# A graph kernel's gather pass over groups of 512 edges in place of 1024, with rings of eight smaller slots

## What is computed

```python
x = x + L0(h)     # sum over edges of h[src] * W
x = x + L1(h)     # two mean aggregations with weights between
x = x + L2(h, edge_attr)
x = x + L3(h)     # mean over edges of h[src] @ W.T + b
```

```python
eh = edge_h @ W_fcr.T
alpha = _segment_softmax(eh, dst, N)
z = h[src]
agg = jax.ops.segment_sum(alpha * (z + eh), dst, num_segments=N)
h_new = jnp.where((deg > 0)[:, None], agg + h @ loop_W, h)
return jax.nn.relu(h_new)
```

## Time and profile before

| | us |
|---|---|
| median of 3 runs (lowest, highest) | 6717.57 (6715.99, 6721.05) |
| the profiled execution, its own time | 6711.77 |
| its span, first to last instruction | 6709.9 |
| gather pass, first to last gather issue | 4275.6 to 6428.4 |
| busy over the span: PE, PE weight loads, DVE, ACT, POOL | 5183.6, 4649.6, 4620.1, 3754.5, 3317.2 |

### The profile page before, as it was taken

One profiled execution on the slowest core, in us unless ns is written; L12 is line 12 of the kernel. 1 busy time (PEld: TensorE's weight loads), 2 busy tenths in 40 slices (PEclk: granted clock), 3 DMA queues, 4 the chain that ended last, 5 costly groups with the idle time before them and its releaser, 6 DMA issues.

```text
span 6709.9 us, 129361 instructions
## 1 busy us (share of the span) xinstructions
PE 5183.6 (77%) x47386; PEld 4649.6 (69%) x47387; DVE 4620.1 (69%) x6392; ACT 3754.5 (56%) x3088; POOL 3317.2 (49%) x3412
## 2 busy tenths in 40 slices
PE   0046548888888849999989999656888878888886
PEld 0011137777777749999989999656777767777776
DVE  9846648888888877888878888434555555555554
ACT  0101137777777757887867878203545545454565
POOL 0477777777777720000010000377777777777730
PEclk9978769999999979999999999878999999999998
DMA  9998997777778766666666666335777767776785
GB/s 347 353 233 262 280 289 241 237 241 237 238 242 242 226 149 186 200 195 192 197 175 193 202 195 195 107 82 126 157 150 157 153 140 153 150 155 149 159 139 113
DMA packets 1691085, 1314.11 MB, mean 196 GB/s; under 512 B 920210, under 2 KB 1555091, under 8 KB 1690031
## 3 DMA queue, kind: packets, MB, share of 16 engines
q1 hardware_dynamic: 872085, 948.47, 48.1%
q10 hardware_dynamic: 705808, 299.82, 19.2%
q0 software_dynamic: 112592, 57.76, 5.3%
HBM read 833.36 MB, written 311.54 MB: 171 GB/s over the span
## 4 chain that ended last, share of the span: by engine, by line
PE 41%; DVE 6%; ACT 5%; issue 5%; DMA 3%; POOL 3%; DVEq 2%; SPq 0%; ACTq 0%; POOLq 0%
PE pair L1719 23%; PE pair L1839 8%; PE wide L1863 6%; ACT u L1613 3%; POOL u L1200 3%; ACT batch L1613 2%; DVE u L967 1%; DMA extra<-hi_b,tsel 1%; DMA u<-zrows,stage 1%; PE wide L1902 1%; DMA u<-cells 1%; DVEq L421 1%; DVE batch L1032 1%; ACT u L1450 0%; DVE u L623 0%
## 5 line engine op out<-in xcount | busy, mean ns | idle before, releaser
L1719 PE MATMUL pair<-tab,u 128*128 128x192 bf16 (+1 forms) x29106 | 2527.5, 247 | 114.9 <-ACT u L1450 110.6
L1719 PEld LDWEIGHTS pair<-tab,u 128*128 128x128 bf16 x29106 | 2459.7, 98 | 134.6 <-ACT u L1450 113.7
L1450 ACT ACTIVATE u<-u 128x1792 bf16<-128x1792 uint8 (+1 forms) x1360 | 2270.6, 1701 | 388.2 <-PE pair L1719 209.2
L1200 POOL DMA_INDIRECT u<-zrows,stage x1664 | 1608.7, 967 | 1329.0 <-DMA zrows<-batch 784.0
L1165 POOL DMA_INDIRECT cells<-val,idx x1664 | 1618.3, 973 | 742.9 <-issue 492.5
L623 DVE TENSOR_REDUCE u<-u 128x1792 bf16<-128x1792 uint8 (+1 forms) x838 | 1673.5, 2020 | 351.1 <-PE pair L1719 250.6
L1839 PE MATMUL pair<-u 128*128 x4880 | 937.5, 350 | 412.7 <-DVE u L967 395.8
L1839 PEld LDWEIGHTS pair<-u 128*128 128x128 f32 x4880 | 854.1, 203 | 488.4 <-issue 487.0
L1613 ACT ACTIVATE u<-u 128x1792 bf16<-128x1792 uint8 x317 | 524.9, 1684 | 316.0 <-PE wide L1863 309.5
L1679 PE MATMUL wide<-u,wbd 128*128 128x512 f32 x840 | 514.0, 702 | 194.1 <-DVE u L732 102.6
L1863 PE MATMUL wide<-u 128*128 128x193 bf16 x5544 | 521.4, 246 | 37.4 <-ACT u L1613 31.1
(11 more groups left out here) (284 smaller groups left out, 4363.4 us busy)
## 6 DMA issues: line engine op xcount, KB each, us to landing
u<-cells SPq DMA_DIRECT2D x2100, 224.0 KB, 3.1
cells<-zt SPq DMA_DIRECT2D x100, 1568.0 KB, 15.7
u<-in_ea SPq DMA_DIRECT2D x420, 256.0 KB
ex_d<-u ACTq DMA_DIRECT2D x420, 256.0 KB
u<-ex_d SPq DMA_DIRECT2D x208, 512.0 KB
u<-gate_d SPq DMA_DIRECT2D x420, 64.1 KB
u<-gate_d ACTq DMA_DIRECT2D x420, 64.0 KB
cells<-val,idx POOLq DMA_INDIRECT x1664
```

The source lines that it names most:

```text
L1200: pool.indirect_dma_start(out=ring3[:, slot, k, :], out_offset=None, in_=zrows, in_offset=bass.IndirectOffsetOnAxis(ap=stage[:, st, c:c + ...
L1450: return S.activation(to, of, ACT.Copy)
L1719: mm = M(acc(p, t // 2 * 2 + b)[:, 0:width], ring[:, q % nr, (b * CK + k) * P:(b * CK + k + 1) * P], table[:, j, 0:width], start=j == 0 an ...
```

## The change

`CH` goes from 8 to 4 and with it the group from 1024 to 512 edges (416 groups); the rings `ring3` and `exr` get eight slots of half the size, so that they hold the same 32 columns; SP loads seven groups ahead in place of three, POOL waits for the landing four groups back in place of two. A group's halves become two columns. `SG`, `GET_AT` and `ADD_AT` are doubled, so they name the same edges. In the scatter the half groups of four columns, which were the unit of three in flight (`DEEP`), become the groups themselves. Two small tables change their place (`below`, `ends`).

```diff
-CH = 8
+CH = 4
 GE = CH * P
 G = -(-E // GE)
-SLOTS = 4
-SG = 8
+SLOTS = 8
+SG = 16
...
-XR = 4
+XR = 8
...
-        shared = sb("shared", [P, max(GPK * T, STEPS + 1)])
-        below = shared[0:GP, 0:GPK * T].rearrange("p (a t) -> p a t", a=GPK)
-        ends = shared[:, 0:STEPS + 1]
+        below = hi_b[0:GP, 0:GPK * T].rearrange("p (a t) -> p a t", a=GPK)
+        ends = sb("ends", [P, STEPS + 1])
...
-        GET_AT, ADD_AT = 20, 60
+        GET_AT, ADD_AT = 40, 120
...
-                for h in range(2 * g, 2 * g + 2):
-                    if h >= DEEP:
-                        done(h - DEEP)
-                    for k in range(CH // 2):
-                        c = h * (CH // 2) + k
-                        pool.indirect_dma_start(out=spots, out_offset=bass.IndirectOffsetOnAxis(ap=idx[:, c:c + 1].bitcast(u32), axis=0),
-                                                in_=val[:, c:c + 1], in_offset=None).then_inc(scat[h % DEEP], 16)
-
-            def done(h):
-                pool.wait_ge(scat[h % DEEP], CH // 2 * 16 * (h // DEEP + 1))
-                if h % 2:
-                    pool.sem_inc(scat_done, 1)
+                if g >= DEEP:
+                    done(g - DEEP)
+                for c in range(g * CH, (g + 1) * CH):
+                    pool.indirect_dma_start(out=spots, out_offset=bass.IndirectOffsetOnAxis(ap=idx[:, c:c + 1].bitcast(u32), axis=0),
+                                            in_=val[:, c:c + 1], in_offset=None).then_inc(scat[g % DEEP], 16)
+
+            def done(g):
+                pool.wait_ge(scat[g % DEEP], CH * 16 * (g // DEEP + 1))
+                pool.sem_inc(scat_done, 1)
...
-                if g >= 2:
-                    pool.wait_ge(landed[(g - 2) % SLOTS], CH * 16 * ((g - 2) // SLOTS + 1))
+                if g >= 4:
+                    pool.wait_ge(landed[(g - 4) % SLOTS], CH * 16 * ((g - 4) // SLOTS + 1))
```

More of the change, by code:

```diff
@@ L1179, in _ @@
                     list_add(0, g - ADD_AT)
-            for h in range(2 * G - DEEP, 2 * G):
-                done(h)
+            for g in range(G - DEEP, G):
+                done(g)
             heads_add(0)
```

## The result

The changed kernel takes **6939.4 us** (median of 6 runs, 6933.4 to 6945.1), the kernel before beside it 6719.3 (6 runs, 6715.7 to 6728.8): a ratio of 1.0329, 95% interval [1.0318, 1.0339]. It is slower by 220 us, as forecast (6937).

What follows compares the result with a forecast made beforehand. Turns 1 to 6 were taken as bound by the consumers' one-group-at-a-time chain, turn 0 by POOL. 380.9 - 109.2 - 44.5 - 4 - 3 = +220 us on 6717.6 gave 6937 us, range 6880 to 7020.

Steps and rivals of the forecast that it cites:

- The chain step: Gather pass, turns 1 to 6: each further group of a tile costs 2.42 us through SP, DVE and PE, before 2.95.
- SP's issue takes 0.36 and I leave it: Within a step, SP's load issue keeps its 0.36 us; if it halved, a step were 0.18 less.
- The steps in all: Turns 1 to 6: 272 steps of 2.42 us replace 94 of 2.95, +380.9 us.
- ends of the pass: Last seven groups of the gather pass need no load ahead: four steps about 1 us shorter, -4 us.
- The closing group: Each of 84 tiles' last group in turns 1 to 6: eight PE passes instead of 16, -109.2 us.
- The opening: Opening group to first further group, 84 tiles: DVE's product and compare shrink by 0.53 us, -44.5 us.
- Turn 0: First turn of the gather pass: stays bound by POOL's gathers, only the last group's work shrinks, -3 us.
- the list additions come nearer together: Scatter pass: additions some 6.6 us apart, but one lands in 4.24 us, so no wait, 0 us.
- Rival 1: POOL or PE paces turns 1 to 6, SP's release does not gate: faster, 6660 to 6675 us; chance 0.07.
- Rival 2: No change: added steps hide under something else, such as ACT's casts; 6705 to 6731 us, chance 0.03.
- Rival 3: PE idles in each step and loses its clock in the groups: slower still, 7030 to 7300 us; chance 0.07.
- Rival 4: Small DVE operations save nothing: step stays 2.95 us, opening unchanged, 7126 us; chance 0.03.

Runs made afterwards that it cites:

- e1: Changed kernel with SP's load issued one group later in its loop, six groups ahead in place of seven: 6752.8 us, ratio to before 1.0053.
- e4: Changed kernel with each load of expanded edges issued from SP as two DMAs of half the size, same bytes: 7082.9 us, ratio to before 1.0543.
- e3: Changed kernel with the scatter pass's eight list additions behind every second group of four scatters, not every group: 6928.1 us, ratio to before 1.0311.
- e5: Changed kernel with four slots and four rows of edge inputs in place of eight and eight: 6973.0 us, ratio to before 1.0379.

## Why the prediction was right, and where its terms were off

**The chain step** (2.42 us forecast, 2.41 measured) and its parts. By the tile above: PE's start to the product 5460.11 to 5461.57 = 1.46 (forecast 0.62 + 0.84), product to compare 0.34 (0.61 - 0.265), compare to PE 0.61 (0.42 + 0.20). What doesn't depend on the size did stay, and the two operations shrank as the straight line said. e1 and e4 show that the part through SP is on the path: moving the load out takes 0.72 us from each step, a second load adds 0.52. "SP's issue takes 0.36 and I leave it" was right, too: a load of half the elements is issued in 0.360 us, as in the earlier trace rows.

**The steps in all**: +380.9 forecast, 662.8 - 288.4 = +374.4 measured. The 94 steps of before cost 288.4 us, not 277.3: I multiplied by the typical 2.95, and their mean is 3.07, since six of them, one a turn and all in its eighth tile, behind a norm chain, take 4.5 to 5.3. The 272 came to 662.8, not 658.2. The **ends of the pass** (-4, four steps about 1 us shorter) are in these 662.8: the last five steps of the pass take 1.69 to 1.73, some 0.7 less than the others, -3.6 in all.

**The closing group**: -109.2 forecast, 117.7 - 226.2 = -108.5 measured. **The opening**: -44.5 forecast, 331.6 - 383.3 = -51.7 measured, 0.62 us each in place of 0.53. In the tile above the path from product to PE falls by 0.57 (1.53 in the earlier trace rows, 0.96 now), and the product itself starts 0.16 earlier behind the opening group's start (1.87 in the earlier trace rows, 1.71 now); the second part I had not counted, and what brings it is not settled.

**Turn 0** had -3 and gave -0.8. **POOL's wait for slots** grew off the path, as forecast; **loop entries** at 0 and the **clock** at 0 held: the step came out at its forecast, and the clock at 0.94 as before.

**The step that failed**: "the list additions come nearer together ... but one lands in 4.24 us, so no wait: 0". The last scatter came 12.8 us later, and e3 shows the additions to be the cause of nearly all of it. The addition of the earlier trace rows belongs to a later list, in another stage. Here the first five land in 7.75 to 9.03 us, longer than the spacing of some 6.6 us that I had worked out. The trace of before could have told it: there a scatter that stands 8.23 us behind an addition is put down to that addition's landing.

```profile
902.12 1.59 POOL L1140 DMA_INDIRECT extra<-hi_b,tsel  x1 [0.30 <-issue]
910.35 0.96 POOL L1165 DMA_INDIRECT cells<-val,idx  x1 [0.30 <-DMA extra<-hi_b,tsel]
```

The scatters beside it are not what makes the difference. Before, the eight additions of this list all stand among scatters, 12 us apart, and by their semaphore the first four land in 8.0 to 8.8 us, the last four in 4.7 to 5.9. What falls between them is the load on the DMA engines (trace of before, columns as in the earlier trace rows; the share of busy DMA time is the last but one, and a full load reads about 1):

```profile
915.00:930.00 15.00, 3.67 (x10) 2.14 (x10) 3.81 (x5) 2.45 (x4) 11.65 (x12) 0.61 1.02 343
...
955.00:970.00 15.00, 9.12 (x26) 5.10 (x24) 8.57 (x12) 3.65 (x6) 11.65 (x12) 0.50 0.77 221
```

In the changed kernel, too, the last three, from 932.9 on, land in 6.0, 3.5 and 3.6 us, and nothing waits for them. No run changes the load alone, so it is a reading of the traces.

So the sum against the profiled execution was 10 us short (220 for 230), and the median came out nearly on the forecast because the two profiled executions lie 10 us further apart than the medians: that part of the agreement is luck.

**The rivals.** Rival 1 asked for a step below 1.61 us for any gain. With the late load the step is 1.69 in the median and 1.76 in the mean (479.9 / 272), and turns 1 to 6 take 1891 us, 30 more than before; with four pieces it is 1.60 and 1.68 (456.2 / 272), and they take 1866, 5 more. The point at which it turns was about right; the changed kernel stands far on the other side. That PE is the fullest engine decided nothing: its passes fell and the time rose. Rival 2 went with the time itself, 220 us longer. Rival 3 did not come about: with PE idle for 0.85 us ahead of a step, as in the tile above, the granted clock of turns 1 to 6 is 0.94, as before. The Trainium skill (TensorE: Matmul & The Clock Gate, "A second HAM failure mode: psum-queue depth-cycling") tells of a kernel in which short idle times of PE between groups made the clock swing between its two levels. These idle times brought no such loss. In e5, behind 4.19 us without a weight load, the clock did fall (last section). Rival 4 is refuted by the two groups of 0.427 and 0.417 us.

## What to carry to other kernels

Where several engines pass one group at a time from hand to hand, lay a step out as its chain, and ask of each link whether it depends on the group's size: halving the group multiplies the links that don't (here 94 steps became 272). Look then at what a passing engine does between two releases, here a wait and a load that served a group seven ahead; moving it behind the next release took 187 us off the changed kernel and 24 off the kernel before. And price a transfer from a row of the same stage: an addition of the same kind landed in 4.2 us in a later stage and in 8 to 9 here, while the DMA engines were full.

## What the runs showed of the hardware

- SP's issue of one plain DMA takes 0.36 us whether it moves 512 KB (before) or 256 KB (changed); of two back to back (e4) the first takes 0.36 and the second 0.47, in the median.
- POOL's list additions in the scatter pass of before land in 8.0 to 8.8 us while the DMA engines are full (share 1.00 to 1.07), and in 4.7 to 5.9 once the share has fallen to 0.68 to 0.83.
- An elementwise instruction of VectorE that does not read the result of the one ahead starts before that one has ended: 0.34 us from product to compare, for a product of 0.43 (e1). Making the product 0.26 us shorter therefore brought an opening only 0.09 us.
- In e5 the weight loads of one group take 1.27 us and those of the next, behind 4.19 us without a load, 2.42: full clock and half, 2.4 and 1.2 GHz. The busy time by stretch of these 22 us (columns as in the earlier trace rows) has the granted clock at 1.00 and then at 0.84, without any norm chain:

```profile
5984.00:5996.00 12.00, 8.72 (x64) 7.79 (x63) 4.92 (x16) 0.00 (x0) 8.96 (x11) 1.00 0.39 94
5996.00:6006.00 10.00, 4.28 (x18) 3.70 (x17) 2.18 (x6) 0.00 (x0) 7.56 (x9) 0.84 0.34 84
```
